# Moving the third Gelu chunk ahead of the last exponentials on ScalarE

## The reference, cut to what matters

```
x = x + 0.5 * local_ffn(layernorm(x))     # "first" stage
x = x + relative_position_attention(layernorm(x))
x = x + 0.5 * local_ffn(layernorm(x))     # "third" stage
x = x + 0.5 * experts(layernorm(x))       # guest of a "first" stage
x = x + state_space(layernorm(x))
x = x + 0.5 * experts(layernorm(x))       # guest of a "third" stage

def layer(x, ...):                        # local_ffn is two of these
    q, k, v = split(shift_token(x) @ wqkv)            # 8 heads of 64
    q, k = rotary(l2norm(q) * qs, l2norm(k) * ks)
    sim = einsum(q * 8, k of this and the last window of 64), masked
    x = x + softmax(sim) @ v @ wo
    h = layernorm(shift_token(x)) * lg + lb
    a, g = split(h @ w1 + b1)                         # 341 + 341 columns
    return x + (a * gelu(g)) @ w2 + b2                # erf Gelu
```

## Time and profile before

| | |
|---|---|
| median of three runs | 5003.36 us (4996.8 to 5006.51) |
| the profiled execution | 5002.3 us, of which its span 5000.5 us |
| busy: PE, DVE, ACT, POOL | 4101.9, 3000.7, 2788.3, 2053.4 us |
| busy share of the span | 82%, 60%, 56%, 41% |
| granted TensorE clock, mean | 0.92 of full speed |
| L1564 (Gelu): table loads | 96 |
| L1446 (Exp): table loads | 48 |

### The profile page before, as it was taken

One profiled execution on the slowest core, in us unless ns is written; L12 is line 12 of the kernel. 1 busy time (PEld: TensorE's weight loads), 2 busy tenths in 40 slices (PEclk: granted clock), 3 DMA queues, 4 the chain that ended last, 5 costly groups with the idle time before them and its releaser, 6 DMA issues. The chain is left out here.

```text
span 5000.5 us, 55506 instructions
## 1 busy us (share of the span) xinstructions
PE 4101.9 (82%) x17410; PEld 2440.5 (49%) x17410; DVE 3000.7 (60%) x5750; ACT 2788.3 (56%) x6185; POOL 2053.4 (41%) x1328
## 2 busy tenths in 40 slices
PE   6887788888878888887987979879788888888846
PEld 3445454455545454454644545445454445445412
DVE  4326567556576574765657656666557647477464
ACT  4465457455575465664565646755557555565432
POOL 2113245444264351653436434444336435264334
PEclk9799999999989999998998989989899999999867
DMA  3020013011031111211121111301113111121212
GB/s 100 1 84 1 27 45 118 29 45 38 32 118 42 33 46 62 80 48 33 51 85 56 49 34 49 110 31 47 35 39 118 33 41 44 53 91 46 74 52 73
DMA packets 188862, 274.38 MB, mean 55 GB/s; under 512 B 23448, under 2 KB 102900, under 8 KB 188532
## 3 DMA queue, kind: packets, MB, share of 16 engines
q1 hardware_dynamic: 186340, 268.72, 16.8%
q10 hardware_dynamic: 2192, 1.70, 0.1%
HBM read 215.54 MB, written 54.79 MB: 54 GB/s over the span
## 5 line engine op out<-in xcount | busy, mean ns | idle before, releaser
L592 POOL TENSOR_TENSOR work<-work 128x512 f32<-128x512 f32 x512 | 671.4, 1314 | 1140.1 <-DVE work L652 1074.1
L1344 POOL TENSOR_TENSOR work<-work,minus_half 128x8 f32<-128x8 f32 x256 | 467.3, 1839 | 592.3 <-DVE work L1327 590.8
L560 PE MATMUL psum<-work,w_up 128*128 128x512 f32 x1024 | 557.5, 628 | 91.9 <-DVE work L652 87.1
L1446 ACT ACTIVATE work<-psum,work 128x128 f32<-128x128 f32 (+1 forms) x1024 | 391.7, 395 | 431.6 <-DVE work L1468 431.2
L652 DVE SCALAR_TENSOR_TENSOR work<-work,psum 128x512 f32<-128x512 f32 x528 | 361.4, 685 | 425.5 <-ACT work L584 424.5
L584 ACT ACTIVATE work<-psum 128x512 f32<-128x512 f32 x528 | 315.5, 598 | 466.4 <-PE psum L560 455.7
L566 PE MATMUL psum<-work,w_down 128*128 128x512 f32 x1024 | 536.6, 606 | 5.1 <-POOL work L592 5.1
L1411 PEld LDWEIGHTS psum<-work 128*128 128x128 f32 x3072 | 400.8, 202 | 60.9 <-issue 60.2
L1411 PE MATMUL psum<-work 128*128 128x64 f32 x3072 | 418.8, 282 | 4.1 <-DVE work L1478 4.1
L1275 PE MATMUL psum<-wqkv,xn 128*128 128x512 f32 x768 | 380.0, 622 | 35.0 <-DVE xn L1573 28.9
L902 DVE TENSOR_TENSOR_SCAN work<-work,psum 128x256 f32<-128x256 f32 x512 | 323.1, 673 | 73.2 <-issue 35.1
(11 more groups left out here) (210 smaller groups left out, 8682.7 us busy)
## 6 DMA issues: line engine op xcount, KB each, us to landing
work<-expert_weight_rows SPq DMA_DIRECT2D x1024, 128.0 KB, 2.9
position_scores<-work SPq DMA_DIRECT2D x64, 768.0 KB, 3.5
work<-position_scores SPq DMA_DIRECT2D x64, 512.0 KB, 3.8
work<-state_readout_rows SPq DMA_DIRECT2D x72, 256.0 KB, 4.3
rows<-state_readout_rows SPq DMA_DIRECT2D x32, 256.0 KB, 3.9
sq<-state_readout_rows SPq DMA_DIRECT2D x24, 256.0 KB, 4.2
rows<-in_L_attn_q SPq DMA_DIRECT2D x8, 256.0 KB, 3.4
expert_weight_rows<-work SPq DMA_DIRECT2D x16, 128.0 KB, 2.3
```

Source lines behind the costliest of these rows:

```text
L560: nc.tensor.matmul(UP, b.w_up[:, p * 128:(p + 1) * 128], self.xn, start=True, stop=True).then_inc(self.up, 1)
L592: pool.tensor_tensor(h, h, self.weights[p % self.SLOTS], ALU.mult).then_inc(self.gated, 1)
L1344: pool.tensor_tensor(half, half, b.minus_half[:].broadcast_to([128, LH]), ALU.pow).then_inc(self.inv_norm, 1)
L1446: ins = self.nc.scalar.activation(out[:, x, -n:] if t else out[:, x], self.scores(m)[:, x], ACT.Exp, bias=self.neg_max[i % 2][:, slot:slot ...
```

## The change

In the two slots that hold attention and a mix, ACT took the exponentials of round 5 (score group 5 of the pass) and then the Gelu of chunk 2. Now, in round 5 alone, the Gelu stands first. Nothing else is edited.

```
                 for r in R:
+                    if r == 5:
+                        project(act, self.mix_scalar, 0, r, self.MIX_AT)
                     self.attend_scalar(act, 1, r)
-                    project(act, self.mix_scalar, 0, r, self.MIX_AT)
+                    if r != 5:
+                        project(act, self.mix_scalar, 0, r, self.MIX_AT)
                     beside.scalar(act, due(6, r))
...
                 for r in R:
+                    if r == 5:
+                        project(act, self.mix_scalar, 2, r, self.MIX_AT)
                     self.attend_scalar(act, 3, r)
-                    project(act, self.mix_scalar, 2, r, self.MIX_AT)
+                    if r != 5:
+                        project(act, self.mix_scalar, 2, r, self.MIX_AT)
                     beside.scalar(act, due(6, r))
```

## The result

The changed kernel takes 5057.35 us (median of four runs, 5046.99 to 5066.08), the kernel before 5004.93 us (4996.80 to 5008.76). The ratio is 1.0106 with a 95% interval of 1.0094 to 1.0118: slower by 52 us. The profiled execution took 5046.99 us (span 5045.2), 44.7 us more than the profiled execution of the kernel before (5002.3, span 5000.5). Its mean granted clock is 0.924; the one of before has 0.921.

A forecast was written before the change was run, and what follows sets the result against it. PE's gapless queue was taken as the bound, its transposes needing the exponentials ahead of the down-projection. Delays of 35.8 and 7.4 us made 43.2 us on 5002.3, plus 1.1 to the median: forecast 5046, range 5032 to 5060.

The forecast's parts named there:

- The saved loads bring nothing: ACT, one table load less in each of 32 slots: 41.1 us less ACT work, counted as no gain by itself.
- The earlier Gelu brings nothing: ACT, round 5: Gelu of chunk 2 starts 2.14 us earlier, but PE reaches L1541 only at 619.32; gain nothing.
- The exponentials are late by 1.85 us, and 0.69 of it is covered: PE before L1400: 1.28 us a slot in 28 guest slots (35.8 us), 1.85 in four of group 0 (7.4 us).
- The delay lasts: Next slot's DVE-bound stretch: DVE's work shifts with PE, so nothing is taken back and the whole delay counts.
- The clock in group 0: Four slots without guest, behind L1400: longer low clock could cost 0 to 7 us; taken as 0, 7 kept for range.
- The clock elsewhere: PE's later waits, shifted 5 us a group against the clock's changes: 7 us in either direction, in the range only.
- The sum: Whole kernel: 35.8 us for guest slots plus 7.4 for group 0, 43.2 us on the profiled execution's 5002.3.
- The rival that put a fall of the clock directly behind the new wait in all slots with a guest: PE in 28 guest slots: two waits bring the low clock, 1.7 us more each, 48 us in all, 5094; chance 4%.
- The rival of a faster kernel by fewer table switches: ACT in rounds 5 and 6: saved loads are worth their time, 41.1 us less, 4962; chance 3%.

The follow-up runs named there:

- Tanh base: The kernel before with Tanh in place of Gelu in the mixes of passes 0 and 2, another function, for time alone: 4972.10 us, ratio 0.9938.

## Why the prediction was right, and where its size was off

Forecast 5046 in a range of 5032 to 5060, measured 5057.35: within the range, and 11 us above the forecast, so 52 us where 43 were summed up. By its steps:

- **The saved loads bring nothing.** Right. 41.1 us of ACT's work are gone, and the run with the down-projection first, which keeps that saving, is as fast as the kernel before and not faster.
- **The earlier Gelu brings nothing.** Right: DVE's gate is done 3 us before PE asks for it. The control with L1541 first on the kernel before shows the other side: there the late Gelu costs 0.84 us a slot.
- **The exponentials are late by 1.85 us, and 0.69 of it is covered.** Right: 1.23 us from L1532 to L1400 in 28 slots, as worked out, and 1.88 against 1.85 in group 0, where nothing covers it. The 0.05 us for transposes behind a wait held too (0.66 against 0.60).
- **The delay lasts.** Right: half the change costs about half, in either half, and a stretch at full clock is 1.3 us longer. Each group of two sequences is 5.0 us longer in the mean (596.6 us before, 601.6 after).
- **The clock in group 0.** Mis-sized. I took it at 0, since the matmuls behind the wait "run at the low clock there already". I had read that from one slot of four; the two of pass 3 ran at full clock. The term is 3.5 us in one trace and 5.4 in the other, inside the 7 that I kept for the range.
- **The clock elsewhere.** Mis-sized too. I put it at nothing in the forecast and at 7 us to either side in the range, with no direction. It is 8 us upwards between the slots of pass 1 and pass 3, and -10 and +9 us in the rest of the two traces.
- **The sum.** 43.2 us against 44.7 in the profiled execution looks better than it is: there 47.2 us in the slots and 7.6 of low clock between them meet 10.1 us that the execution gained elsewhere. That is luck; the waits, 44 us, are not.

The rival that put a fall of the clock directly behind the new wait in all slots with a guest is wrong: 1.00 behind all 28. In group 0 it is what happens.

The rival of a faster kernel by fewer table switches, which the Trainium skill's rule in "ScalarE: Activation LUTs" ("Table sets: the hidden batching unit") would have asked for, failed on order and not on the count of switches.

## What to carry to other kernels

A saved instruction is worth something only if someone waits for the engine's next result; read who waits, and what stands first in the waiter's queue. Moving an instruction that must wait ahead of one that is ready turns the wait into the ready one's delay: 1.85 us for 1.28 us of work saved here, and it cost nothing once the waiter had other work in front. Which of several equal instructions is removed matters: the first table load of a slot was worth some 0.9 us, the last one nothing. So change the two queues together: the Gelu first and the down-projection first is even, either one alone costs about 50 us.

## What the runs showed of the hardware that I had not expected

The same program ran at mean granted clocks from 0.915 to 0.924, with times from 5068 to 5047 us, while the kernel before, run beside all of these, stayed between 0.920 and 0.929 and between 4993 and 5016 us. Kernels with PE's pauses moved by a microsecond (the changed one, the control with L1541 first) had the lowest clocks, 0.915 to 0.921 in all executions but one, but the Tanh base was low too, 0.919 to 0.922, without any new pause, and filling the new pause with matmuls gave 0.920 to 0.921.

The same wait did not do the same everywhere. Behind the new wait of 1.07 us in 28 slots with PE busy around it, the clock read 1.00 each time. In group 0, behind 0.90 and 2.79 us of waiting with one group of matmuls between them, it fell (0.67 in the mean behind the wait), and with five unused matmuls in the longer one it read 1.00.

The mean clock of an execution does not say what an edit did to it: the changed kernel's execution at 0.924 had the low clock in 13 of the 14 stretches shown above, against 6 in the kernel before at 0.921, and made up for it elsewhere. A difference of 10 us in this kernel can thus come with the clock alone, and has to be kept apart from the work of an edit, by comparing stretches at full clock, start to start.
